# A two-layer vision block on one core: first attention's scores in steps of four heads, one block of mean squares, second attention's output read out in three pieces, a shorter first output projection, and a new written-out order

## The reference

```
h   = concat(cls, realFFT(16x16 patches) * freq weights @ proj_w.T + proj_b) + pos_emb   # 197 tokens x 192
# layer 1: attention on layernorm(h), 12 heads of 16
s   = q @ k.T / 4 ; p = softmax(s) ; ctx = p @ v ; h += ctx @ Wo + bo
# layer 2: attention on layernorm(h), 12 heads of 64, q and k layer-normed per head, each
# head's output times a gate (2 shared heads, the top 2 of 10 routed ones, from softmaxes of h)
o   = softmax(ln(q) @ ln(k).T / 8) @ v ; h += (gates * o) @ proj_w + proj_b
```

## Time and profile before

| | us |
|---|---|
| runs (3): median, lowest, highest | 5536.16, 5532.93, 5536.67 |
| span of the profiled execution, first to last instruction | 5532.4 |
| PE busy in that span | 5344.4 (97%) |
| DVE, ACT, POOL busy | 4923.8, 4327.1, 2985.7 |
| granted TensorE clock, mean share of full speed | 0.997 |

### The profile page before, as it was taken

One profiled execution on the slowest core, in us unless ns is written; L12 is line 12 of the kernel. 1 busy time (PEld: TensorE's weight loads), 2 busy tenths in 40 slices (PEclk: granted clock), 3 DMA queues, 4 the chain that ended last, 5 costly groups with the idle time before them and its releaser, 6 DMA issues.

```text
span 5532.4 us, 202492 instructions
## 1 busy us (share of the span) xinstructions
PE 5344.4 (97%) x63024; PEld 4563.7 (82%) x63024; DVE 4923.8 (89%) x16193; ACT 4327.1 (78%) x17409; POOL 2985.7 (54%) x3206
## 2 busy tenths in 40 slices
PE   3999999999999999999999999999999999999998
PEld 2788888888888888888888888888888888888887
DVE  5899999999999999999999999999999999999996
ACT  1777887887888788788778878877887887887786
POOL 0555555555555555555555555555555555555554
PEclk9999999999999999999999999999999999999999
DMA  2000000000000000000000000000000000000000
GB/s 72 18 22 18 17 21 17 18 17 21 18 17 21 17 18 17 21 18 17 21 18 17 20 18 18 17 21 18 17 21 17 18 17 21 18 17 21 18 17 6
DMA packets 60519, 106.93 MB, mean 19 GB/s; under 512 B 8076, under 2 KB 33944, under 8 KB 60128
## 3 DMA queue, kind: packets, MB, share of 16 engines
q1 hardware_dynamic: 60456, 106.12, 6.2%
HBM read 86.72 MB, written 19.37 MB: 19 GB/s over the span
## 4 chain that ended last, share of the span: by engine, by line
PE 94%; DVE 4%; issue 1%; ACT 0%; POOL 0%; SPq 0%; DVEq 0%; DMA 0%; POOLq 0%; ACTq 0%
PE bank L491 82%; PE bank L672 10%; PE bank L529 2%; DVE qk L898 1%; DVE qkn L996 1%; SPq L403 0%; ACT p L733 0%; DMA bp<-in_bp 0%; ACT pq L771 0%; POOL pq L475 0%; DVEq L902 0%; DVEq L1025 0%; DVE wqk_mean L804 0%; DVEq L992 0%; DVE nmax L903 0%
## 5 line engine op out<-in xcount | busy, mean ns | idle before, releaser
L475 POOL TENSOR_TENSOR pq<-pq,gn 99x788 f32<-99x788 f32 x768 | 1153.3, 1502 | 914.0 <-DVE gn L1011 913.9
L771 ACT ACTIVATE pq<-bank,nmax 99x197 f32<-99x197 f32 x3072 | 1300.1, 453 | 291.6 <-DVE nmax L1002 291.6
L733 ACT ACTIVATE p<-bank,nmax 99x197 f32<-99x197 f32 x3072 | 1323.1, 467 | 112.0 <-DVE nmax L903 97.3
L484 POOL TENSOR_TENSOR qkb<-qkn,ln_b 128x396 f32<-128x396 f32 x768 | 639.5, 847 | 1164.0 <-DVE qkn L996 1151.4
L777 ACT ACTIVATE pT<-bank 99x394 f32<-99x394 f32 x1536 | 767.6, 518 | 259.4 <-PE bank L672 256.4
L903 DVE TENSOR_REDUCE nmax<-bank 99x2 f32<-99x394 f32 x1536 | 843.2, 563 | 113.9 <-PE bank L491 101.7
L1002 DVE TENSOR_REDUCE nmax<-bank 99x2 f32<-99x394 f32 x1536 | 827.2, 559 | 25.7 <-PE bank L491 10.7
L733 ACT ACTIVATION_READ_ACCUMULATOR p<-bank,nmax 99x1 f32 x3072 | 762.6, 248 | 0.0
L491 PE MATMUL bank<-x2T,wqkc 128*128 128x198 f16 (+1 forms) x7680 | 752.5, 248 | 1.0 <-ACT p L733 0.7
L672 PE MATMUL bank<-ident,pq 99*99 99x99 f32 (+1 forms) x6144 | 725.3, 253 | 7.7 <-ACT pq L771 5.2
L771 ACT ACTIVATION_READ_ACCUMULATOR pq<-bank,nmax 99x1 f32 x3072 | 720.7, 235 | 0.0
(11 more groups left out here) (148 smaller groups left out, 10116.0 us busy)
## 6 DMA issues: line engine op xcount, KB each, us to landing
xa<-in_xa SPq DMA_DIRECT2D x128, 300.1 KB
xb<-in_xb SPq DMA_DIRECT2D x128, 300.1 KB
out_tokens<-res SPq DMA_DIRECT2D x128, 74.2 KB
out_tokens<-res SPq DMA_DIRECT2D x128, 73.5 KB
p<-in_wq SPq DMA_DIRECT2D x1, 1152.0 KB
pT<-in_wk SPq DMA_DIRECT2D x1, 1152.0 KB
qkc<-in_basis SPq DMA_DIRECT2D x1, 661.5 KB
sq<-in_wq SPq DMA_DIRECT2D x1, 576.0 KB
```

What stands on the lines that cost most here:

```text
L475: nc.gpsimd.tensor_tensor(pair, pair, factor, op=ALU.mult).then_inc(s_sc.up(), 1)
L484: nc.gpsimd.tensor_tensor(qkb[:, t], qkn[:, t % QKN_SLOTS], ln_b[:].unsqueeze(2).to_broadcast([128, 2, TP]), op=ALU.add).then_inc(s_qk.up( ...
L733: last = nc.scalar.activation(p1[0:TC, h, c, :], psum("s1", h)[0:TC, c * T:c * T + T], ACT.Exp, bias=nmax1[:, c, h:h + 1], accum_out=sum1[ ...
L771: last = nc.scalar.activation(pq[0:TC, h % SLOTS, c, 0:T], psum("s2", h)[0:TC, c * T:c * T + T], ACT.Exp, bias=nmax2[:, h, c:c + 1], accum ...
```

## The change

1. `s1` takes four heads a step, in the four 32-row groups of the array and four banks; three steps of 16 matmuls per image instead of six of eight. The number of matmuls stays 48.
2. `ms` becomes one step of 12 matmuls that waits for all six squares.
3. `o2` puts four heads into one bank, two beside two: three steps of eight matmuls instead of six of four, and three copies on ACT and three subtractions on DVE of 128x394 instead of six of 128x197.
4. `vs` is written by POOL instead of DVE, twice side by side, and so `ctx` comes out with each head's 16 rows doubled. ACT's float16 copy is scaled per row by 1 in one of the two and by 0 in the other (`low_half`); DVE subtracts that copy from both, and the 128 rows then hold high and low halves stacked. `wo` needs 12 matmuls instead of 18.
5. The four written orders (PE, DVE, ACT, POOL) are new.

```diff
+    half = np.zeros((GROUP, 2, E1), np.float32)
+    half[:, 1] = 1.0
+    c["low_half"] = half.reshape(128, 1)
...
-3:tok@1 0:pT_6@5 1:rstd0@0 0:pT_7@4 0:pT_8@2 1:rstd1@6 0:pT_9@5 0:pT_10@3 0:pT_11@2 0:o2_2@7 0:o2_3@3 0:o2_4@0
...
+0:pT_8@5 0:pT_9@3 3:qk1_1@7 1:rstd1@5 1:s2_0@61 3:qk1_2@3 1:rstd2@7 0:pT_10@4 1:rstd3@5 0:o2_1@2 0:pT_11@3 3:s1_4@5076
+1:v2_0@4 1:rstd4@3 3:ctx0@2 0:o2_2@1 1:s2_2@05 1:v2_1@4 1:v2_2@2 3:s1_8@1763 1:v2_3@4 1:pT_0@0 0:proj@2 1:rstd5@4
...
+def last_of(engine, steps):
+
+    order = list(steps_of(engine))
+    return max(steps, key=lambda s: next((-ahead, i) for i, (ahead, *step) in enumerate(order) if tuple(step) == s))
...
+            def v1_scaled(img, g):
+
+                hs = slice(GROUP * g, GROUP * g + GROUP)
+                pool.wait_ge(*read_out(img, "v1", 0))
+                pool.wait_ge(*s_rsum1.at(img, g + 1))
+                for c in range(2):
+                    n = TC - c
+                    last = nc.gpsimd.tensor_tensor(
+                        vs1[0:n, c, hs, :].rearrange("p h (d e) -> p h d e", d=2),
...
+                last.then_inc(s_vs.up(), 1)
...
-                if h % 2:
-                    return
-                heads = (h, h + 1)
-                assert uses["s1", h][0] != uses["s1", h + 1][0]
-                if h % GROUP == 0:
-                    pe.wait_ge(*read_out(img, "qk1", h // GROUP))
+                g, heads = h // GROUP, range(h, h + GROUP)
+                assert len({uses["s1", i][0] for i in heads}) == GROUP
+                pe.wait_ge(*read_out(img, "qk1", g))
                 for i in heads:
                     pe.wait_ge(*room_for(img, "s1", i))
...
-                    for n, (x, w) in enumerate(((0, 0), (1, 0), (0, 1))):
+                    for w in range(2):
                         for g in range(3):
-                            last = mm(o[0:TC, c * D:c * D + D], ctxT[:, g, x, c * TC:c * TC + TC], wo1[:, w, g, :], n + g == 0, n + g == 4)
+                            last = mm(o[0:TC, c * D:c * D + D], ctxT[:, g, c * TC:c * TC + TC], wo1[:, w, g, :], w + g == 0, w + g == 3)
...
+                pe.wait_ge(*s_sq.at(img, 6))
+                for u in range(H):
...
+                pe.wait_ge(*read_out(img, *last_of("act", [("pT", h) for h in range(4 * k, 4 * k + 4)])))
+                for i in range(2):
+                    for c in range(2):
+                        for j in range(2):
+                            h = 4 * k + 2 * i + j
+                            last = mm(o[64 * j:64 * j + 64, i * T:i * T + T], v2[:, c, E2 * h:E2 * h + E2], pT[:, h, c, :], c == 0, c == 1)
...
-                nc.scalar.activation(ctxT[:, g, 0, 0:T], psum("ctx", g)[:, 0:T], ACT.Copy).then_inc(s_ctxh.up(), 1)
+                nc.scalar.activation(ctxh[:, g, 0:T], psum("ctx", g)[:, 0:T], ACT.Copy, scale=low_half[:, 0:1]).then_inc(s_ctxh.up(), 1)
...
-                step(V.reciprocal(rsum1[:, :, hs], sum1[:, :, hs]), img, "ctx", g + 1)
-                dve.wait_ge(*read_out(img, "v1", 0))
-                for c in range(2):
-                    n = TC - c
-                    last = V.tensor_tensor(vs1[0:n, c, hs, 0:E1],
...
+                V.reciprocal(rsum1[:, :, hs], sum1[:, :, hs]).then_inc(s_rsum1.up(), 1)
...
-            def o_low(img, t):
-                dve.wait_ge(*s_oh.at(img, t + 1))
-                V.tensor_tensor(oT[:, t, 1, 0:T], psum("o2", t)[:, 0:T], oT[:, t, 0, 0:T], op=ALU.subtract).then_inc(free("o2", t), 1)
+            def o_low(img, k):
+                pair = slice(2 * k, 2 * k + 2)
+                dve.wait_ge(*s_oh.at(img, k + 1))
+                V.tensor_tensor(oT[:, pair, 1, 0:T], psum("o2", k)[:, 0:2 * T].rearrange("p (i n) -> p i n", i=2), oT[:, pair, 0, 0:T],
+                                op=ALU.subtract).then_inc(free("o2", k), 1)
```

More of the change, by code:

```diff
@@ L131 @@
     "pe": """
-3:tok@1 0:pT_6@5 1:rstd0@0 0:pT_7@4 0:pT_8@2 1:rstd1@6 0:pT_9@5 0:pT_10@3 0:pT_11@2 0:o2_2@7 0:o2_3@3 0:o2_4@0
[L133 to L136, removed]
+0:s2_6@37 0:s2_8@42 2:ctx1@1 2:ctx2@6 1:gl@0 1:qk0@5 0:pT_2@1 2:wo@6 3:tok@3 0:pT_3@7 1:qk1@0 1:qk2@6 0:pT_4@0 1:qk3@5
@@ L137 @@
+1:qk4@3 1:qk5@6 0:pT_5@1 3:x1T@4 0:s2_10@05 1:ms0@3 3:v1@7 0:pT_6@2 0:pT_7@0 3:qk1_0@4 0:o2_0@6 1:rstd0@3 3:s1_0@1420
+0:pT_8@5 0:pT_9@3 3:qk1_1@7 1:rstd1@5 1:s2_0@61 3:qk1_2@3 1:rstd2@7 0:pT_10@4 1:rstd3@5 0:o2_1@2 0:pT_11@3 3:s1_4@5076
+1:v2_0@4 1:rstd4@3 3:ctx0@2 0:o2_2@1 1:s2_2@05 1:v2_1@4 1:v2_2@2 3:s1_8@1763 1:v2_3@4 1:pT_0@0 0:proj@2 1:rstd5@4
+1:pT_1@7 2:x2T@1 1:s2_4@60
 """,
     "dve": """
-3:fold 1:var2 0:gr5 0:ol1 2:wo 1:rstd0 1:rstd1 3:tok 0:ol2 0:ol3 0:ol4 3:nx1 0:ol5 1:s2_0 1:s2_1 1:gate3 1:s2_2 1:s2_3
@@ L140 @@
-1:v2_0 3:x1T 2:nx2 1:rstd2 3:qk1_0 0:proj 3:s1_0 3:s1_1 3:s1_2 1:s2_4 3:qk1_1 3:s1_3 1:v2_1 1:gr0 1:v2_2 1:s2_5 1:v2_3
-1:gr1 2:x2T 3:s1_4 3:qk1_2 1:rstd3 3:s1_5 3:ctx0 3:s1_6 1:gr2 1:s2_6 1:s2_7 1:rstd4 3:s1_7 1:rstd5 2:gl 3:s1_8 3:ctx1
-1:gr3 3:s1_9 2:gate1 3:s1_10 1:s2_8 3:s1_11 1:s2_9 2:gate2 3:ctx2 1:s2_10 1:gr4 3:cl0 3:cl1 3:cl2 1:ol0 1:s2_11
+0:gr1 0:gr2 0:s2_6 2:cl1 2:cl2 3:fold 0:s2_7 0:s2_8 1:gl 2:wo 0:s2_9 3:tok 1:gate1 3:nx1 0:gr3 0:gr4 0:s2_10 3:x1T
+0:s2_11 1:gate2 1:var2 3:qk1_0 1:rstd0 3:s1_0 3:s1_1 0:ol0 0:gr5 3:s1_2 3:s1_3 3:qk1_1 1:rstd1 1:rstd2 1:s2_0 3:qk1_2
@@ L143 @@
+1:rstd3 1:s2_1 3:ctx0 0:ol1 3:s1_4 3:s1_5 3:s1_6 3:s1_7 1:v2_0 1:rstd4 1:gate3 3:cl0 1:gr0 1:s2_2 0:ol2 1:v2_1 1:v2_2
+3:s1_8 3:s1_9 1:v2_3 2:nx2 3:s1_10 3:s1_11 1:s2_3 1:rstd5 3:ctx1 0:proj 1:s2_4 3:ctx2 2:x2T 1:s2_5
 """,
     "act": """
-3:x1T 1:s2_2 3:qk1_0 1:s2_3 3:qk1_1 3:s1_0 3:s1_1 3:s1_2 1:s2_4 3:qk1_2 3:s1_3 2:x2T 1:s2_5 3:v1 1:pT_0 3:s1_4 1:pT_1
-2:qk0 3:s1_5 2:qk1 3:s1_6 1:s2_6 2:qk2 1:pT_2 1:s2_7 3:s1_7 2:gate0 3:s1_8 2:qk3 2:qk4 2:qk5 3:s1_9 1:pT_3 3:s1_10
-3:s1_11 1:s2_8 1:s2_9 3:ctx0 3:ctx1 1:o2_0 3:ctx2 2:var0 2:var1 1:pT_4 1:s2_10 1:pT_5 1:s2_11 1:o2_1 1:pT_6 1:pT_7
@@ L148 @@
-1:pT_8 1:pT_9 1:pT_10 1:o2_2 1:pT_11 1:o2_3 1:o2_4 1:o2_5 2:s2_0 2:s2_1
+2:s1_7 0:s2_2 2:s1_8 2:s1_9 0:pT_0 2:s1_10 2:s1_11 0:pT_1 0:s2_3 1:x2T 0:s2_4 0:s2_5 2:ctx1 2:ctx2 0:s2_6 0:pT_2 1:qk0
+0:s2_7 0:pT_3 1:gate0 1:qk1 0:s2_8 1:qk2 0:pT_4 1:qk3 0:s2_9 1:qk4 1:qk5 3:x1T 0:s2_10 0:pT_5 1:var0 1:var1 0:s2_11
+3:qk1_0 0:pT_6 0:pT_7 3:v1 0:o2_0 0:pT_8 3:s1_0 0:pT_9 3:qk1_1 3:s1_1 3:s1_2 3:qk1_2 3:s1_3 1:s2_0 0:pT_10 0:o2_1
+0:pT_11 1:s2_1 3:s1_4 3:s1_5 3:ctx0 0:o2_2 3:s1_6
 """,
     "pool": """
-3:root1 1:bias2 3:h1b 1:h2c 2:h2b 1:sc0 1:sc1 1:bias3 2:sq0 1:sc2 2:sq1 1:bias4 1:bias5 2:sq2 2:sq3 2:sq4 1:sc3 2:sq5
@@ L234, in build_vit_block @@
         mask1 = sb("mask1", [128, 1])
+        low_half = sb("low_half", [128, 1])
         freq_h = sb("freq_h", [72, 2])
@@ L608, in gl, with mean_square @@
                 last.then_inc(full("gl", 0), 1)
[L610 to L615, removed]
+            def mean_square(img, _):
+                pe.wait_ge(*room_for(img, "ms", 0))
+                pe.wait_ge(*s_sq.at(img, 6))
+                for u in range(H):
                     q = 32 * (u % 4)
-                    last = mm(psum("ms", 0)[q:q + 32, 0:TP], sel_var[:, u, :], sq[:, u // 2, u % 2, :], t == 0, t == 2)
-                if t == 2:
-                    last.then_inc(full("ms", 0), 1)
+                    last = mm(psum("ms", 0)[q:q + 32, 0:TP], sel_var[:, u, :], sq[:, u // 2, u % 2, :], u < 4, u >= 8)
+                last.then_inc(full("ms", 0), 1)
             def qk(img, t):
```

52 lines of the change are left out of this document (24 added, 28 removed).

## The result

The changed kernel took 6280.7 us (median of 4 runs, 6278.5 to 6284.3) where the kernel before took 5536.4 beside it: a ratio of 1.1347, 95% interval 1.1331 to 1.1363. It is slower by 744 us; 3.7% faster was forecast. In the middle of the run one image takes 47.79 us, where it took 42.01: 5.78 x 128 = 740 us, so the whole loss recurs in every image. Of `e9_v2_first`, further down, only the profiled execution is used: its three others took 9.4 to 11.8 ms, for a reason that stays open.

What follows compares the result with a forecast made beforehand. PE was taken as the bound: its work falls 1.33 to 40.1 us per image, plus 0.25 of waits gives 40.35, saving 211 us over 128 periods; with 10 for filling, 5330 us, eight-in-ten range 5245 to 5440.

Steps and rivals of the forecast that it cites:

- What bounds the kernel: Whole kernel before: PE is the bound, busy 41.45 of 42.00 us per image; DVE, at 38.06, could become it.
- The PE terms: PE's list per image: -1.07 scores, -0.49 projection, +0.10 squares and `ctx`, 0 `o2`, -0.17 `s2`, +0.30 entries; sum -1.33 us.
- A step of four heads: Scores on PE: 0.50 us a step, bounds 0.47 and 0.69; three steps 1.50 instead of 2.57.
- the rival that weight loads set its pace: Four-head scores: 16 weight loads need 0.68, a step 0.80 us, period 41.25, time 5446; chance 0.03.
- the mean squares with `ctx`: Mean-square and `ctx` steps on PE: 3.37 us per image after the change instead of 3.25, so +0.1.
- the run of three `s2`: `s2_4`, `s2_6` and `s2_8` in sequence on PE: 2.18 us, with three further pairs standing alone.
- the order's -0.17: `s2` on PE: the new order makes one run of three and three alone, 4.70 us instead of 4.87.
- Will the others keep up?: Other engines per image: DVE 35.8 us, POOL 26.9, ACT only loses work, against PE's 40.1; so they keep up.
- Waits, 0.25: PE's waits per image: the 0.56 for `qk` goes, new ones lie between 0 and 1.0; 0.25 us taken.
- the four places that I named: Possible new PE waits at `s1_4`, `ctx0`, the block of mean squares and `s2_6`; together between 0 and 1.0 us.
- the one on the slower side: Four-bank wait at `s1_8` for banks ACT frees: at 3.5 us late, 2.4 of wait, time 5606; chance 0.04.
- Filling: Pipeline filling and emptying: `tok` to `proj` takes 3.7 passes of the list instead of 3.4; 10 us added.

Runs made afterwards that it cites:

- e9_v2_first: Kernel before with stacked ctx rows and 12 matmuls for the first output projection, plus v2_1 moved on PE ahead of the first scores; 5504.1 us (one run).
- e2: Changed kernel with the six squares of an image made by ACT out of PSUM, none by POOL; 5556.7 us, ratio 1.0039 to the kernel before.
- e1: Changed kernel with 38 more matmuls of 192 columns, results unused, ahead of PE's wait for the first layer's normalised rows; 5988.6 us (one run).

## Why the prediction was wrong, point by point

**What bounds the kernel:** PE, 97% busy, was rightly read for the kernel before.

**The PE terms** of the steps that were changed were mostly right, where the clock is full. A step of four heads: 0.50 forecast, 0.48 measured (2534.13 to 2534.61 in the changed kernel, first fence below); the rival that weight loads set its pace is out. `wo`: 1.00 forecast, 0.98 to 0.99 measured. `o2`: 1.49 a step, 1.48 to 1.49. Two were too small: the mean squares with `ctx` are 3.56 in e2 (1.27, 1.48 and 0.81) for 3.37, and the run of three `s2` is 2.54 for 2.18, so that the order's -0.17 became +0.19. Both end in an idle of PE that is too short for the views to name (0.13 us behind the run, 0.06 behind the squares), so they hold a wait each and not a higher price alone.

```profile
2534.13 0.55 PE L516 MATMUL bank<-qk 32*99 32x197 f16 x16
2534.61 1.02 PE L516 MATMUL bank<-wv,x2T 128*99 128x384 f16 x5
```

```profile
2506.91 2.41 PE L512 MATMUL bank<-qkb 64*99 64x197 f32 x24
2509.45 1.55 PE L512 MATMUL bank<-p,vs 128*32 128x197 f32 x32
2510.93 0.64 PE L512 MATMUL bank<-wgate,x2T 128*99 128x14 f16 x10
2511.42 1.03 PE L512 MATMUL bank<-x2T,wqkc 128*128 128x198 f16 x10
2512.65 0.59 PE L688 MATMUL bank<-ident,pq 99*99 99x99 f32 x4 [0.20 <-DVE ctxT L1027]
```

The second fence is e2: the run of three `s2` lasts from 2506.91 to 2509.45, two `ctx` from there to 2510.93; the last two rows are read under the waits.

**"Will the others keep up?" is the step that failed.** It compared sums of busy time: DVE 35.8 of 40.1, POOL 26.9 of 40, "so it has room in sum". Both sums take an instruction's length as given. POOL's hardly moved from that estimate (26.1 of 47.8) and DVE's became 41.3 instead of 35.8, because `x` and `gn` wait inside their own instructions while POOL works, and count as busy. The step should have laid POOL's new list beside DVE's. It is plain there that `root1` releases DVE's `x` and POOL goes on to four squares at once; and the trace of before already held the price: of the two products of `vs`, alike but for one row, the first had a mean of 405 ns and the second of 213. Told apart by whether POOL was at work when they began, the products of that trace take 496 and 216. I read 405 and 213 as two prices, not as one instruction with and without POOL beside it.

The Trainium skill states the mechanism ("SBUF — State Buffer", Who interferes with whom): a VectorE copy, cast or tensor_scalar in a two-port mode, or an instruction with two SBUF inputs against a GpSimd one that reads SBUF, shares an exclusive port pair with GpSimd, and whoever issues second blocks for the whole of the other's instruction. The trace agrees on which instructions are hit: `x` (a tensor_scalar) and `gn` (two SBUF inputs, a mean of 871 ns where POOL was at work when it began and 163 where not) are, while `qkn`, with an input from PSUM, takes 416 and 418 ns in the changed kernel with POOL at work and without. For `x` it is harsher in one respect: the page has the second one blocked for one instruction, and here `x` did not get in between the squares but stood for all four, 3305 ns.

**Waits, 0.25:** of the four places that I named, none became more than 0.2; the wait of 3.47 came at a fifth, the transposes, where none had been. Of the 7.44 us by which the period missed 40.35, 3.47 are this wait and 2.54 the low clock behind it (2.35 by e1). The remaining 1.4 is nearly what e2, which has neither, misses: 1.65. The windows view of e2 tells how that is made up:

```profile
2500.00:2542.00 42.00, 41.20 (x488) 34.04 (x487) 37.30 (x118) 36.18 (x142) 21.20 (x26) 1.00 0.06 18
```

PE is idle 0.80 us of an image where 0.25 was allowed for, and busy 41.20 where 40.1 was forecast. The idle stands at five places: 0.62 that the trace names (0.20 for `ctx`'s rows, 0.25 for ACT's `qkc`, 0.17 at a scores step) and the two short ones above. And a wait costs PE more than its idle, which the forecast had no term for: the ten products of `x2T` at 2511.42 take 1.03 us up to the wait, where ten products of that size are 0.86 when the next step follows at once. At about 0.17 in each of five places, where the kernel before had one, that is an estimated 0.7 of the 1.1 us of excess busy time; what the rest is stays open.

**The rivals:** the one on the slower side had the right form, a step that comes 3.5 us late, but at another place (`s1_8`, which did not wait), and without the clock. The chance of 0.94 for faster rested on the list of places where something could be late having been complete.

**Filling:** span less 128 periods is 156 us before and 166 in the changed kernel: +10, as forecast. In e2 it is 182, so that the agreement is in part luck.
